# Attention inside a fused layer: k's rotation and the half-precision splits of v and of the transposed probabilities move to GpSimd, and every engine's order is rewritten

## The reference, cut to what matters

```
q = h @ dequant(q_codes)      # 32 heads of 128
k = h @ dequant(k_codes)      # 8 heads, each used by 4 heads of q
v = h @ dequant(v_codes)
q, k = rope(q), rope(k)
attn = softmax(q k^T / sqrt(128) + causal mask)
x = x + (attn @ v) @ dequant(o_codes)
x = x + ffn(cond2(x))         # gated low-rank experts over a base matrix
```

## Time and profile before

| | |
|---|---|
| median of 3 runs | 1815.58 us (1813.62 to 1817.37) |
| the profiled execution | 1816.87 us, its span 1815.0 us |
| mean granted TensorE clock | 0.987 |
| PE / DVE / ACT / POOL busy | 1717.1 / 1576.7 / 1268.1 / 745.9 us |
| attention, first matmul to last `add_out` | 86.2 to 1573.6 us of the span |

### The profile page before, as it was taken

The page is one execution under the profiler, slowest core; times in us unless marked ns, Lnnn a source line. Parts: engine busy times, 40 slices in busy tenths (PEclk is TensorE's granted clock), DMA queues, the critical chain, the costliest instruction groups (busy, mean ns, idle before and its releaser), DMA issues. The chain is left out here.

```text
span 1815.0 us, 37518 instructions
## 1 busy us (share of the span) xinstructions
PE 1717.1 (95%) x14847; PEld 920.5 (51%) x14911; DVE 1576.7 (87%) x2359; ACT 1268.1 (70%) x2154; POOL 745.9 (41%) x557
## 2 busy tenths in 40 slices
PE   8989999999999999999999999999999998589998
PEld 7834444444444444444444444444444444156665
DVE  5579999999999999999999999999999998389997
ACT  2358878887888788888887888788888886522222
POOL 1035444544454445444544454445444444133332
PEclk9899999999999999999999999999999999889999
DMA  7100000000000100000000000000000000412221
GB/s 270 34 9 25 13 30 2 24 13 31 1 24 13 30 1 25 13 30 1 24 13 30 1 24 13 30 2 25 13 1 1 1 1 1 151 47 77 75 82 47
DMA packets 23769, 56.81 MB, mean 31 GB/s; under 512 B 6968, under 2 KB 7480, under 8 KB 22320
## 3 DMA queue, kind: packets, MB, share of 16 engines
q1 hardware_dynamic: 23600, 54.44, 9.2%
HBM read 45.50 MB, written 8.93 MB: 30 GB/s over the span
## 5 line engine op out<-in xcount | busy, mean ns | idle before, releaser
L620 PE MATMUL banks<-o_hl,w_o 128*128 128x512 f16 x2048 | 573.4, 382 | 25.5 <-ACT banks L904 17.3
L904 ACT ACTIVATE banks<-banks,ratios 128x512 f32<-128x512 f32 x768 | 490.0, 657 | 143.7 <-PE banks L620 143.1
L540 PE MATMUL banks<-hT,w_q 128*128 128x512 f16 x2048 | 538.5, 381 | 12.1 <-POOL rope_k L142 4.8
L900 ACT ACTIVATE banks<-banks,ratios 128x512 f32<-128x512 f32 x768 | 475.2, 661 | 90.9 <-PE banks L540 90.8
L840 POOL TENSOR_TENSOR q_f<-q_f,q_sin 128x1024 f32<-128x1024 f32 x128 | 300.8, 2350 | 374.1 <-DVE q_f L724 193.5
L620 PEld LDWEIGHTS banks<-o_hl,w_o 128*128 128x128 f16 x2048 | 161.7, 97 | 320.5 <-ACT banks L904 174.1
L540 PEld LDWEIGHTS banks<-hT,w_q 128*128 128x128 f16 x2048 | 196.3, 98 | 245.3 <-issue 21.3
L724 DVE TENSOR_TENSOR q_sin<-banks,rope_q 64x1024 f32<-64x1024 f32 x256 | 312.9, 1222 | 7.2 <-POOL q_f L840 1.5
L715 DVE TENSOR_SCALAR banks<-banks,ratios 128x512 f32<-128x512 f32 x192 | 145.0, 755 | 97.7 <-PE banks L555 97.7
L568 PE MATMUL banks<-w_v,hT 128*128 128x128 f16 x3072 | 193.1, 219 | 0.0
L568 PEld LDWEIGHTS banks<-w_v,hT 128*128 128x128 f16 x3072 | 177.1, 98 | 21.9
(11 more groups left out here) (123 smaller groups left out, 1787.5 us busy)
## 6 DMA issues: line engine op xcount, KB each, us to landing
codes<-in_codes SPq DMA_DIRECT2D x40, 512.0 KB, 3.7
accT<-in_xT SPq DMA_DIRECT2D x8, 1024.0 KB, 12.7
x_f<-in_x SPq DMA_DIRECT2D x32, 256.0 KB, 2.9
out<-res SPq DMA_DIRECT2D x32, 256.0 KB, 2.1
v_s<-in_v_scales SPq DMA_DIRECT2D x8, 256.0 KB, 4.5
hT<-aggb_rows SPq DMA_DIRECT2D x1, 2048.0 KB, 13.6
hT<-in_base_T SPq DMA_DIRECT2D x1, 1024.0 KB, 5.9
aggw_rows<-agg_sb SPq DMA_DIRECT2D x1, 512.0 KB, 2.7
```

The costliest lines, as they stand in the source:

```text
L540: mm = pe.matmul(banks[:, tile], w.q[:, n[2], kt * RF * HD + tile * HD:kt * RF * HD + (tile + 1) * HD], hT[:, kt, hp, t0:t0 + CHUNK], star ...
L620: mm = pe.matmul(o_bank(tile), w.o[:, p[2], h * D + tile * P:h * D + (tile + 1) * P], o_hl[:, op, h], start=h == 0 and op == 0, stop=op == ...
L900: act.activation(banks[:, tile], banks[:, tile], ACT.Copy, scale=w.ratios[:, n[0], tile, kt:kt + 1]).then_inc(q_scaled[tile], 1)
L904: act.activation(o_bank(tile), o_bank(tile), ACT.Copy, scale=w.ratios[:, p[0], RF + tile, h:h + 1]).then_inc(o_scaled[tile], 1)
```

## The change

On DVE `rotate_k_sin`, `rotate_k_cos` and `v_low` go, and `softmax_T` transposes 512 columns of single precision (`sc` to the new `pT`) and not 1024 of half precision. On ACT `p_high` goes and a new `move_k` copies k out of its bank into `k_f`; `move_v` now writes single precision into the new `v_f`. POOL gets the two rotations of k (from `k_f`, the sine part from the other half of the partitions), `v_high`, `v_low` and `p_high`; `p_low` stays there, behind the transpose. Projections of v start when `move_k` is done, projections of k when `move_v` is done.

```diff
+    v_f = sb("v_f", [P, CT, HD])
-    p_hl = sb("p_hl", [P, 2, CHUNK], F16)
+    pT = sb("pT", [P, CHUNK])
...
# PE: project_k(n, 0)
-                    pe.wait_ge(v_ready, at(n))
+                    pe.wait_ge(v_moved, at(n))
# PE: project_v(n, 0)
-                pe.wait_ge(k_cos_done, at(n) + 1)
-                pe.wait_ge(k_sin_done, at(n) + 1)
+                pe.wait_ge(k_moved, at(n) + 1)
# PE: values(p, 0)
-                pe.wait_ge(probs_T, at(p) + 1)
+                pe.wait_ge(p_ready, at(p) + 1)
# DVE: softmax_T
-            dve.wait_ge(p_ready, at(i) + 1)
+            dve.wait_ge(probs, at(i) + 1)
...
-            dve.transpose(pT_hl[:].rearrange("p a t -> p (a t)"), p_hl[:].rearrange("p a t -> p (a t)")).then_inc(probs_T, 1)
+            dve.transpose(pT[:], sc[:]).then_inc(probs_T, 1)
# POOL
+        def rotate_k_sin(n):
+            pool.wait_ge(k_moved, at(n) + 1)
+            if at(n):
+                pool.wait_ge(k_ready, at(n))
+            pool.wait_ge(q_ready[0], at(n) + 1)
+            for h in range(2):
+                src = slice(64 * (1 - h), 64 * (2 - h))
+                ins = pool.tensor_tensor(by_s(k_f[64 * h:64 * (h + 1), 1]), by_s(k_f[src, 0]), table(w.rope_k[:, n[2], 1], src), ALU.mult)
+            ins.then_inc(k_sin_done, 1)
+        def rotate_k_cos(n):
+            pool.wait_ge(k_sin_done, at(n) + 1)
+            pool.tensor_tensor(by_s(k_f[:, 0]), by_s(k_f[:, 0]), table(w.rope_k[:, n[2], 0]), ALU.mult).then_inc(k_cos_done, 1)
...
+        def p_high(i):
+            pool.wait_ge(probs_T, at(i) + 1)
...
+            pool.tensor_copy(pT_hl[:, 0], pT[:]).then_inc(p_hi, 1)
+        def v_high(n):
+            pool.wait_ge(v_moved, at(n) + 1)
...
+            pool.tensor_copy(v_hl[:, n[1] % 2, 0], v_f[:]).then_inc(v_hi, 1)
+        def v_low(n):
+            pool.wait_ge(v_hi, at(n) + 1)
+            pool.tensor_tensor(v_hl[:, n[1] % 2, 1], v_f[:], v_hl[:, n[1] % 2, 0], ALU.subtract).then_inc(v_ready, 1)
...
-            pool.tensor_tensor(p_hl[:, 1], sc[:], p_hl[:, 0], ALU.subtract).then_inc(p_ready, 1)
+            pool.tensor_tensor(pT_hl[:, 1], pT[:], pT_hl[:, 0], ALU.subtract).then_inc(p_ready, 1)
# ACT
+        def move_k(n):
+            act.wait_ge(k_psum, KT * at(n) + KT)
+            if at(n):
+                act.wait_ge(scores_psum, at(n))
+            act.activation(k_f[:, 0], kv_bank, ACT.Copy).then_inc(k_moved, 1)
...
-            act.activation(v_hl[:, n[1] % 2, 0].rearrange("p j d -> p (j d)"), kv_bank, ACT.Copy, scale=1 / WSCALE).then_inc(v_hi, 1)
+            act.activation(v_f[:].rearrange("p j d -> p (j d)"), kv_bank, ACT.Copy, scale=1 / WSCALE).then_inc(v_moved, 1)
```

More of the change, by code:

```diff
@@ L630, in body @@
             if i:
+                project_v(i, 0)
+            if n:
+                project_q(n, 1, 0)
+                project_q(n, 0, 1)
+            if p:
+                values(p, 1)
+            if i:
                 project_v(i, 1)
             if n:
-                project_q(n, 0, 1)
+                project_q(n, 0, 2)
+                project_q(n, 1, 1)
                 project_q(n, 2, 0)
-                project_q(n, 1, 1)
+                project_k(n, 0)
+            if p:
+                output(p, 1, 0)
+                output(p, 0, 0)
+            if n:
                 project_q(n, 3, 0)
+                project_k(n, 1)
             if p:
[L638 to L643, removed]
+                output(p, 1, 1)
+                output(p, 0, 1)
             if i:
@@ L759, in softmax_T @@
         def softmax_T(i):
-            dve.wait_ge(p_ready, at(i) + 1)
+            dve.wait_ge(probs, at(i) + 1)
             if at(i):
-                for half in range(2):
-                    dve.wait_ge(pv_psum[half], 2 * at(i))
-            dve.transpose(pT_hl[:].rearrange("p a t -> p (a t)"), p_hl[:].rearrange("p a t -> p (a t)")).then_inc(probs_T, 1)
[L766 to L769, removed]
+                dve.wait_ge(p_ready, at(i))
+            dve.transpose(pT[:], sc[:]).then_inc(probs_T, 1)
         def out_low(p, b):
@@ L786, in body @@
         def body(n, i, p):
+            if i:
+                turn_cos(i, 1)
             if p:
@@ L790, in body @@
             if i:
-                v_low(i)
-            if n:
-                scale_k(n, 0)
+                turn_sin(i, 1)
             if p:
@@ L800, in body @@
                 scores_T(i)
+                softmax_max(i)
             if n:
                 scale_k(n, 2)
[L803 to L807, removed]
+            if p:
+                add_out(p, 1)
+                add_out(p, 0)
             if i:
@@ L819, in body @@
             if n:
-                turn_cos(n, 1)
+                turn_cos(n, 0)
             if p:
+                add_out(p, 3)
                 add_out(p, 2)
-                add_out(p, 3)
-            if n:
-                turn_sin(n, 1)
         program(body)
@@ L879, in body @@
             if i:
+                add_k(i)
                 add_q(i, 1)
-                add_k(i)
+            if i and i[0] < NKV - 1:
+                dequantize(i)
+            if i:
                 shift(i)
+                v_high(i)
                 normalize(i)
+                v_low(i)
+                p_high(i)
                 p_low(i)
@@ L886, in body @@
                 add_q(n, 0)
-            if i and i[0] < NKV - 1:
-                dequantize(i)
+                rotate_k_sin(n)
+                rotate_k_cos(n)
         program(body)
@@ L916, in move_v @@
             act.wait_ge(v_psum, at(n) + 1)
-            if at(n) >= 2:
-                for half in range(2):
-                    act.wait_ge(pv_psum[half], 2 * at(n) - 2)
-            act.activation(v_hl[:, n[1] % 2, 0].rearrange("p j d -> p (j d)"), kv_bank, ACT.Copy, scale=1 / WSCALE).then_inc(v_hi, 1)
-        def p_high(i):
-            act.wait_ge(probs, at(i) + 1)
-            act.activation(p_hl[:, 0], sc[:], ACT.Copy).then_inc(p_hi, 1)
+            if at(n):
+                act.wait_ge(v_ready, at(n))
+            act.activation(v_f[:].rearrange("p j d -> p (j d)"), kv_bank, ACT.Copy, scale=1 / WSCALE).then_inc(v_moved, 1)
         def body(n, i, p):
```

133 lines of the change are left out of this document (60 added, 73 removed).

## The result

The changed kernel takes 1750.71 us (median of 4 runs, 1748.08 to 1753.17) beside 1814.6 us for the kernel before (4 runs): a ratio of 0.964 with a 95% interval of 0.963 to 0.966. The prediction was 1749 us, in a range of 1736 to 1789. The profiled execution took 1748.08 us, its span 1746.3.

The account below looks back on a forecast made before the run. TensorE bounds the kernel: 21.33 us of issue and 1.31 of stalls a body, 21.7 in the new order. 118.9 + 62 x 21.7 + 41.4 = 1505.7 saves 67.9 of 1816.87, so 1749 us, range 1736 to 1789.

Parts of the forecast that it names:

- the walk: Engines followed through one body of the new order by start times from the trace: 21.7 us a body.
- the o chains' stalls: TensorE at the body's end: o32 waits 0.06 us, o33 0.07, o23 0.15, as ACT's two scalings follow one another.
- POOL's prices: k's rotation multiplications on POOL: 1.05 to 1.27 us each, 1.27 taken.
- The rival of the crossing: POOL's sine part, reading one partition half and writing the other, costs more; at 2.35 each, 1842 us; chance 0.06.
- POOL's slack: POOL's chain ends before TensorE wants scores at 32.6: 0.45 us to spare at 1.27 a multiplication, 1.1 at 1.05.
- The rival of POOL's chain: Transpose to scores becomes the bound through 0.1 to 0.2 more per hand-over: 22.0 to 22.6 a body, 1768 to 1800; chance 0.15.
- The signs of being wrong: Sine half on POOL over 1.6 us, scores waiting for add_q or add_k every body, q00 and values0 waiting over 0.2.
- The third: Sign of a wrong prediction: scores on TensorE stands waiting for POOL's add_q or add_k in every body.
- The table: dequantize at the front of POOL's body ends TensorE's once-a-head wait for the new table, 1.2 us at most in the queue.
- Fill: First body, from q00 at 86.23 to body 2 at 118.9: 32.7 us, 2.5 before the 121.4 of now.
- the lost cover: At the end, loads behind POOL's clearing no longer land under attention: the end counts 41.4 us, not 39.9.
- Sum: Attention: 118.9 + 62 x 21.7 + 41.4 = 1505.7 against 1573.6, 67.9 us saved, 65.4 in the bodies.

Follow-up runs that it names:

- before_v_on_pool: Kernel before, orders kept, with only v's halves moved to POOL behind add_k and move_v writing single precision: 1817.9 us, ratio 1.001.
- v_split_on_dve: Changed kernel with v's halves as before the change, high half by ACT, low half by DVE behind out_low of block 3: 1794.7 us, ratio 0.988.
- k_rot_on_dve: Changed kernel with k's three rotation multiplications back on DVE behind out_low of block 3, add_k behind add_q(i,1) on POOL: 1890.4 us, ratio 1.041.
- k_rot_dve_early: As k_rot_on_dve, but the multiplications directly behind turn_cos(i,1) on DVE and add_k in front of add_q(i,1) again: 1886.0 us, ratio 1.039.

## Why the prediction was right, point by point

- **The body.** 21.7 was walked, 21.65 measured in the middle and 21.69 on average. DVE's arrivals were right (turn_cos walked to 21.6, measured 21.5). The meetings lie where the walk had them: values0 1.42 us after q00 (1.4), the o chains' stalls 0.06, 0.16 and 0.07 (0.06, 0.07, 0.15, in another order).
- **Why it is shorter.** TensorE needs 21.33; stalls fell from 1.31 to 0.32. before_v_on_pool, v_split_on_dve and k_rot_on_dve show that the relief of DVE counts by where it lets TensorE go on, not by its busy time. That this is so for each part of the change is argued from these three, not tested.
- **POOL's prices.** 1.27 each was right; the lower bound of 1.05 is not met, repeated table or not. The rival of the crossing is refuted.
- **POOL's slack** was mis-sized: 0.45 in the walk, none measured. The rival of POOL's chain was set aside because "the walk has 0.1 for each of them already", the hand-overs inside POOL; its steps have it in front of p_low, the cosine part and add_k, and nowhere else. (Its time at 22.6 us a body would also be 1749 + 62 x 0.9 = 1805, not 1800.) In the trace p_high starts where the walk had it, 1.20 before q00, and the chain ends 10.73 behind q00, 10.5 in the walk; the 0.23 are the 0.17 in front of the sine part and the 0.05 within it. And nothing was taken from POOL's end to the mask's matmul, which is 0.24 to 0.26. So add_q(i,1) was not done 0.4 to 1.1 before the scores, as the prediction said it would be, but only by the length of the hand-over. That this did not show in the time is luck: 0.1 more in the chain would have been 6 us.
- **The signs of being wrong.** The sine half at 1.27 is far from 1.6, and q00 waits for DVE by 0.07 at most. The third, scores waiting for add_q in every body, is a matter of 0.01 us: the prediction stood on its edge.
- **The table.** The wait of the earlier trace rows is gone, as said. But the walk priced dequantize's place by that wait alone; behind the rotations it would have cost 157 us.
- **Fill.** 33.5 us to body 2 (82.91 to 116.44), 32.7 predicted. Missed was what follows: 3.6 us of idle time, and half the clock in body 2, 4.3 us once.
- **End.** From body 64 (1465.3) to the loads' landing 41.6 us, 41.4 predicted, and the loads come last, as the lost cover said. But by 0.5 us and not 1.5: the last sum came after 41.1, 39.9 in the walk. values0 started 0.8 later than walked (21.7 and not 20.9), and from there to the end it took 19.5 and not 19.0.
- **Sum.** Attention lasts 1423.5 us (82.91 to 1506.40), 1419.5 predicted; body 2 is the difference. It saved 63.9 us, by the profiles' attention and by the medians alike, and not the 67.9 predicted. Profiled against profiled 68.8 were saved, since the first stage took 3.3 us less and the last 2.1 less (235.2 against 237.3) with their code unchanged; attention begins anywhere from 81.9 to 88.7 in the fourteen profiles. The 1749 is off by only 1.7 for a reason of the same kind: it was taken from a profiled execution that lay 2.3 above the median of 1814.6, and this made up for part of the 4.0 missed.

## What to carry to other kernels

Work moved off a nearly full engine pays only at the places where another engine waits for that engine; walk one period of the new order with start-to-start times from the trace and look at each meeting. When three engines come within 0.1 us of each other, take every hand-over from a row too, and expect nothing from relieving one of them. When an engine's queue gets longer, small work that stands last in it (here the table) must move ahead first.

## What the hardware showed that was not expected

- A DVE multiplication that reads two operands from SBUF took about 1 us longer where it met a POOL instruction: 1186 ns on average over pairs of which one met it, against 700 with POOL done. The kernel before, where DVE read k from PSUM, has 688.
- Idle stretches of TensorE of 1.7 us (k_rot_dve_early) were followed in about one body of four, and those of 3.6, 4.0 to 4.2 and 8 us each time looked at, by matmuls at half clock (2.74 us for six of 512 columns, 1.46 otherwise); 14 matmuls in the 3.6 us kept it whole. But behind the 2.05 us before k1 in nearly every body of k_rot_on_dve the matmuls ran at full clock (0.60 us for two). The length of the gap alone did not decide it.
- On POOL the cast of 0.61 us made the row 0.55 longer, while the sine part, which waits for the semaphore of the add_q in front of it, started 0.17 us after that ended (0.47 in the late body above).
